# Four graph layers on one core: attention scores from turned gathered rows with 64 target columns, and the edge rows for the scatter assembled in DRAM during the attention

## The reference

```
def _L0_gnn_ref(h, src, dst, Wq, Wk, Wv, Wo, gamma, beta):
    score = jnp.einsum('ehd,ehd->eh', Q[src], K[dst]) / np.sqrt(D)      # H = 4 heads
    attn = jax.nn.softmax(score, axis=1)
    m = V[src] * attn[:, :, None]
    h_new = jax.ops.segment_sum(m, dst, num_segments=n)
    ...
# layer 1: two Chebyshev convolutions, each with two products by the (weighted) adjacency matrix
        return jnp.zeros((n, h.shape[1]), h.dtype).at[row].add(w[:, None] * h[col])
# layer 2: message passing with the 100000 x 64 edge features
    message = jax.nn.relu(node_feats[edge_index[1]] + edge_feats)
    message_reduce = jax.ops.segment_sum(message, edge_index[0], num_segments=num_nodes)
# layer 3: a GAT layer over the same edges
```

## Time and profile before

| | us |
|---|---|
| median of three runs (lowest, highest) | 3534.71 (3491.54, 3550.27) |
| the profiled execution, its span | 3529.8 |
| PE / DVE / ACT / POOL busy in it | 1964.1 / 2235.0 / 1128.3 / 1615.5 |

### The profile page before, as it was taken

The page is one execution under the profiler, slowest core; times in us unless marked ns, Lnnn a source line. Parts: engine busy times, 40 slices in busy tenths (PEclk is TensorE's granted clock), DMA queues, the critical chain, the costliest instruction groups (busy, mean ns, idle before and its releaser), DMA issues. The chain is left out here.

```text
span 3529.8 us, 59565 instructions
## 1 busy us (share of the span) xinstructions
PE 1964.1 (56%) x16222; PEld 1430.6 (41%) x16222; DVE 2235.0 (63%) x4872; ACT 1128.3 (32%) x3658; POOL 1615.5 (46%) x1665
## 2 busy tenths in 40 slices
PE   6844555555555555545766556564545445564487
PEld 5723333333333333334344435453434434554222
DVE  7877777777777777754521112134547557987899
ACT  1144555444444444533210111000001001117544
POOL 1055555555555555553666666645666562000000
PEclk9955555555555555556767677675657657985699
DMA  7912121121212222236222222215544432220000
GB/s 240 364 40 45 42 45 43 43 43 44 45 40 45 42 45 41 45 88 224 65 49 50 50 50 48 60 44 154 147 132 145 127 81 84 85 82 0 0 0 9
DMA packets 399309, 267.13 MB, mean 76 GB/s; under 512 B 321456, under 2 KB 349293, under 8 KB 399073
## 3 DMA queue, kind: packets, MB, share of 16 engines
q1 hardware_dynamic: 306278, 87.81, 11.6%
q10 hardware_dynamic: 41472, 118.96, 9.3%
q0 software_dynamic: 51488, 59.40, 6.7%
HBM read 158.59 MB, written 107.47 MB: 75 GB/s over the span
## 5 line engine op out<-in xcount | busy, mean ns | idle before, releaser
L1254 POOL DMA_INDIRECT sorted_edges<-r_load,r_to x800 | 818.6, 1023 | 544.9 <-SPq L1188 310.2
L807 POOL DMA_INDIRECT hsrc<-h,edges x808 | 775.7, 960 | 593.8 <-PE ps L1004 362.4
L1004 PE MATMUL ps<-AO,hsrc 125*64 125x64 f32 x1616 | 195.9, 316 | 309.9 <-remote 254.3
L1049 PE MATMUL ps<-hot,lo 125*128 125x400 bf16 (+2 forms) x1000 | 272.8, 455 | 100.5 <-DVE hot L866 79.9
L1004 PEld LDWEIGHTS ps<-AO,hsrc 125*64 125x64 f32 x1616 | 180.0, 224 | 345.8 <-issue 345.8
L1031 PE MATMUL ps<-rwin,there 120*125 120x256 bf16 x800 | 183.2, 404 | 235.3 <-DVE there L850 220.0
L875 DVE TENSOR_TENSOR prod<-ps,hsrc 125x1024 f32<-125x1024 f32 x200 | 244.3, 1222 | 105.1 <-issue 101.0
L1572 ACT ACTIVATE w_work<-w_work 128x384 f32<-128x384 f32 (+1 forms) x160 | 85.8, 536 | 701.5 <-DVE w_work L1773 530.4
L866 DVE TENSOR_SCALAR hot<-ramp,small 125x400 bf16<-125x400 int16 x800 | 211.9, 322 | 148.0 <-issue 142.7
L1426 PE MATMUL ps<-R 128*128 128x64 bf16 x3000 | 156.6, 218 | 184.5 <-DVE R L1762 115.9
L1031 PEld LDWEIGHTS ps<-rwin,there 120*125 120x125 bf16 x800 | 145.1, 209 | 274.1 <-issue 274.1
(11 more groups left out here) (412 smaller groups left out, 4187.1 us busy)
## 6 DMA issues: line engine op xcount, KB each, us to landing
w_work<-sorted_edges ACTq DMA_DIRECT2D x42, 1000.0 KB
r_load<-in_edge_attr_dram SPq DMA_DIRECT2D x80, 312.5 KB
dstrow<-dst_rows SPq DMA_DIRECT2D x101, 234.4 KB
sorted_edges<-A ACTq DMA_DIRECT2D x10, 2000.0 KB, 9.7
A<-counts SPq DMA_DIRECT2D x12, 1600.0 KB
counts<-A ACTq DMA_DIRECT2D x4, 4000.0 KB, 29.8
sorted_edges<-A ACTq DMA_DIRECT2D x15, 1000.0 KB, 9.5
hsrc<-h,edges POOLq DMA_INDIRECT x808
```

The lines of the kernel that those rows point to most:

```text
L807: g.indirect_dma_start(out=hsrc[:, s, t, :], out_offset=None, in_=S.h0[:, :], in_offset=bass.IndirectOffsetOnAxis(ap=edges.bitcast(I32)[:, ...
L1004: mm = pe.matmul(sums.rearrange("d (h w) -> d h w", h=H)[:, :, OFF[t]:OFF[t] + SUB], hsrc[0:TP, s, t, :], AO[0:TP, t, :, :], start=(t == 0 ...
L1049: mm = pe.matmul(S.ps[:, at0 + c0:at0 + c1], lo[0:TP, s, t, :], hot[0:TP, t, c0 - k0:c1 - k0], start=(t == FIRST[k]), stop=False, skip_gro ...
L1254: g.indirect_dma_start(out=S.sorted, out_offset=bass.IndirectOffsetOnAxis(ap=to[:, hf, t:t + 1], axis=0), in_=load[:, hf, t, :], in_offset ...
```

## The change

1. **Front.** R is kept transposed (`RT`, f32, 128 partitions x heads x nodes) in place of three bf16 parts. Per block of nodes, two PE products in place of one, one ACT copy in place of two, and no DVE subtractions (`rem`, `low`). The table goes to DRAM as `rt` (6.6 MB in eight DMAs; before 4.8 MB in two). A table `edge_places` of source, target and place per edge (600 KB) replaces two of 800 KB and 400 KB, and `dst_rows` is gone.
2. **Scores.** For each item PE turns the gathered rows (4 transposes), ACT copies them to SBUF (`hT`), and PE multiplies each tile of 125 edges with the 16 x 4 = 64 columns of its 16 nodes (8 f32 products, `rwin` now 128 partitions x 4 x 40 words). DVE picks the edge's own node of 16 with `at` (two products of 125 x 256) and sums over the 16 (one reduction). `there`, `dstrow` and ACT's sums are gone.
3. **Loops.** The attention's loops run over four items (Q = 4), with four slots for `spot`, `edges` and `hsrc`, so POOL may gather up to three items ahead.
4. **Staging.** In the first 20 of its 25 rounds of four items, SP issues `stage_chunk` after each second item: four DMAs from DRAM to DRAM (twice 1250 x 256 B of features and 1250 x 12 B of numbers and places) that assemble one chunk's rows in `staged_edges`.
5. **Scatter.** `bring_half` is one DMA of 128 x 2680 B from `staged_edges`; a row is 67 words, not 80, in the scatter, in the clearing of the table and in the message loop's loads.

```diff
-KW = SP3 * W
+Q = 4
...
-ROW = D + 16
+ROW = D + 3
...
                     c = b - 1
                     act.wait_ge(q["r"], c + 1)
-                    act.copy(R3[:, c, 0, :], S.bank[4 + c % 3][:, 0:H * D]).then_inc(q["hi"], 1)
-                    act.wait_ge(q["rem"], c + 1)
-                    act.copy(R3[:, c, 1, :], rest[:, c % KQ, :]).then_inc(q["mid"], 1)
+                    act.copy(RT[:, :, c * P:(c + 1) * P], S.bank[4 + c % 3][:, 0:2 * P].rearrange("p (k n) -> p k n", k=2)
+                             ).then_inc(q["rt"], 1)
...
+            def kept(b0, b1):
+                act.wait_ge(q["rt"], b1)
+                for half in range(2):
+                    for k in range(2):
+                        act.dma_start(S.rt[half * D:(half + 1) * D, k:H:2, PAD + b0 * P:PAD + b1 * P],
+                                      RT[k * D:(k + 1) * D, :, b0 * P:b1 * P]).then_inc(q["stored"], 16)
...
+                        pe.wait_ge(q["rt"], n - 2)
+                    for k in range(2):
+                        mm = pe.matmul(S.bank[4 + n % 3][:, k * P:(k + 1) * P], Mk[0:D, k * P:(k + 1) * P], HT[0:D, n % KQ, :],
+                                       start=True, stop=True)
+                    mm.then_inc(q["r"], 1)
...
-def bring_half(nc, I, S, sp, c, hf):
-    part = slice(hf * HALF, (hf + 1) * HALF)
-    by_edge = "(p t) f -> p t f"
-    sp.dma_start(S.load[0:TP, hf, :, 0:D], I["edge_attr_64"][bass.ds(c * CE, CE), :].rearrange(by_edge, t=TC)[:, part, :]
-                 ).then_inc(S.landed[hf], 16)
-    with nc.allow_non_contiguous_dma(reason="two node numbers behind each row of features"):
-        sp.dma_start(S.load[0:TP, hf, :, D:D + 2], S.pairs[bass.ds(c * CE, CE), :].rearrange(by_edge, t=TC)[:, part, :]
-                     ).then_inc(S.landed[hf], 16)
-    sp.dma_start(S.to[:, hf, :], S.pos[:, bass.ds(c * TC + hf * HALF, HALF)]).then_inc(S.landed[hf], 16)
+def bring_half(S, sp, c, hf):
+    sp.dma_start(S.load[:, hf, :, :], S.staged[bass.ds(c, 1), hf].rearrange("c p t w -> (c p) t w")).then_inc(S.landed[hf], 16)
+def stage_chunk(nc, I, S, sp, c):
+    by_edge = "(p h t) f -> h p t f"
+    for hf in range(2):
+        rows = S.staged[bass.ds(c, 1), hf, 0:TP].rearrange("c p t w -> (c p) t w")
+        sp.dma_start(rows[:, :, 0:D], I["edge_attr_64"][bass.ds(c * CE, CE), :].rearrange(by_edge, h=2, t=HALF)[hf]).then_inc(S.settled, 16)
+        with nc.allow_non_contiguous_dma(reason="two node numbers and a place behind each row of features"):
+            sp.dma_start(rows[:, :, D:D + 3], S.trip[:, bass.ds((c * 2 + hf) * (HALF * 3), HALF * 3)].rearrange("p (t k) -> p t k", k=3)
+                         ).then_inc(S.settled, 16)
...
-            def line(g, i):
-                sp.wait_ge(q["there"], i + 1)
-                sp.dma_start(dstrow[:, :], S.dst16[bass.ds(g * GE, GE)].unsqueeze(0).to_broadcast([KW, GE])).then_inc(q["dstrow"], 16)
-            with sp.Fori(0, n) as j:
-                for s in range(2):
-                    i = j * 2 + s
-                    g, b = begin(i, s)
-                    sp.wait_ge(q["window_free"], i + 1)
-                    sp.dma_start(rwin[:, s, :], S.r3[bass.ds(b, W)].rearrange("n s c -> (n s) c")).then_inc(q[f"rwin{s}"], 16)
-                    line(g, i)
+            def bring(i, s):
+                b = begin(i, s)
+                sp.wait_ge(q["window_free"], i + 1)
+                sp.sem_inc(q["carrier"], 1)
+                sp.dma_start(rwin[:, s % 2, :, :], S.rt[:, :, bass.ds(b, W)]).then_inc(q[f"rwin{s % 2}"], 16)
+            with sp.Fori(0, C2 // 2) as j:
+                for s in range(Q):
+                    bring(j * Q + s, s)
+                    if s % 2 == 1:
+                        stage_chunk(nc, I, S, sp, j * 2 + s // 2)
+            with sp.Fori(C2 // 2, n) as j:
+                for s in range(Q):
+                    bring(j * Q + s, s)
...
+            sp.wait_ge(S.settled, C2 * 64)
-                bring_half(nc, I, S, sp, 0, hf)
+                bring_half(S, sp, 0, hf)
...
-            with g.Fori(0, n) as j:
-                for s in range(2):
-                    i = j * 2 + s
-                    gather(i + 1, 1 - s, j * 16 + 16 + 16 * s)
+            with g.Fori(0, quads_of(g)) as j:
+                for s in range(Q):
+                    i = j * Q + s
+                    g.wait_ge(landed[s], j * 16 + 16)
+                    g.wait_ge(q["ao_free"], i + 1)
+                    g.sem_inc(q["carrier"], 1)
+                    for t in range(T):
+                        g.indirect_dma_start(out=hsrc[:, s, t, :], out_offset=None, in_=S.h0[:, :],
+                                             in_offset=bass.IndirectOffsetOnAxis(ap=edges.bitcast(I32)[:, s, 4, t:t + 1], axis=0)
+                                             ).then_inc(got[s][t // HT], 16)
...
-                    def products(hf):
-                        v.tensor_tensor(prod[0:TP, :].rearrange("p (t h f) -> p t h f", t=HT, h=H),
-                                        S.ps[0:TP, hf * 1024:(hf + 1) * 1024].rearrange("p (t h f) -> p t h f", t=HT, h=H),
-                                        hsrc[0:TP, s, HT * hf:HT * (hf + 1), :].unsqueeze(2).to_broadcast(four),
-                                        ALU.mult).then_inc(q["scores_free"], 1)
...
-                    keys(0, 4)
-                    products(0)
-                    keys(4, 8)
-                    summed = sums(0)
-                    products(1)
-                    summed = sums(1)
...
+                    v.wait_ge(q["scores"], i + 2)
+                    for r in range(2):
+                        v.tensor_tensor(prod[0:TP, r:T:2, :, :], scores_at(odd, r).rearrange("p (u h w) -> p u h w", u=HT, h=H),
+                                        at[0:TP, r:T:2, :].unsqueeze(2).to_broadcast([TP, HT, H, SUB]), ALU.mult).then_inc(q["scores_free"], 1)
+                    v.wait_ge(q["scores_free"], 2 * i + 6)
+                    own.step(v.tensor_reduce(s4, prod[0:TP, :, :, :], AX.X, ALU.add))
+                    own.step(v.tensor_reduce(top, s4, AX.X, ALU.max))
+                    v.tensor_tensor(s4, s4, over(top, [TP, T, H]), ALU.subtract).then_inc(q["soft"], 1)
...
-            def add(n, hf):
-                act.wait_ge(q["summed"], 2 * n + hf + 1)
-                for c in range(HT * H - BYACT, HT * H):
-                    op = nc.scalar.activation(prod[0:TP, c * D:(c + 1) * D], prod[0:TP, c * D:(c + 1) * D], ACT.Copy,
-                                              accum_out=score[:, hf * HT * H + c:hf * HT * H + c + 1])
-                op.then_inc(q["summed"], 1)
...
-                    add(i, 0)
-                    add(i, 1)
+                for s in range(Q):
+                    act.wait_ge(q["turned"], i + 1)
+                    act.wait_ge(q["scores"], i + 1)
+                    act.copy(hT[:, :, :], S.bank[2 + odd][:, 0:HT * TP].rearrange("p (u e) -> p u e", u=HT)).then_inc(q["moved"], 1)
...
+                    bring_sums(i, j * (Q // 2) + s // 2, odd)
                     act.wait_ge(q["soft"], i + 1)
                     nc.scalar.activation(expo, score, ACT.Exp).then_inc(q["expo"], 1)
-                    rows(i + 1, 1 - s, j * 16 + 16 + 16 * s)
...
-                    pe.wait_ge(q["there"], i + 2)
+                    pe.wait_ge(q["moved"], i + 1)
+                    for u in range(HT):
+                        if u % 2 == 0:
+                            pe.wait_ge(got[s][u // 2], j * (16 * HT) + 16 * HT)
+                        mm = pe.transpose(S.bank[2 + odd][:, u * TP:(u + 1) * TP],
+                                          hsrc[0:TP, s, 2 * u:2 * u + 2, :].rearrange("p t f -> p (t f)"), S.ident[0:TP, 0:TP])
+                    mm.then_inc(q["turned"], 1)
+                    pe.wait_ge(q[f"rwin{odd}"], pair * 16 + 16)
+                    pe.wait_ge(q["scores_free"], 2 * i + 2)
+                    pe.wait_ge(q["moved"], i + 3)
                     for t in range(T):
-                        mm = pe.matmul(S.ps[0:TP, t * 256:(t + 1) * 256], there[:, t * TP:(t + 1) * TP], rwin[:, s, :],
-                                       start=True, stop=True, skip_group_check=True)
-                        if t % HT == HT - 1:
-                            mm.then_inc(q["scores"], 1)
-                    pe.wait_ge(q["scores"], 2 * i + 2)
+                        rows = slice(t % 2 * D, t % 2 * D + D)
+                        mm = pe.matmul(scores_at(odd, t % 2)[:, t // 2 * H * SUB:(t // 2 + 1) * H * SUB], hT[rows, t // 2, :],
+                                       rwin[rows, odd, :, OFF[t]:OFF[t] + SUB], start=True, stop=True, skip_group_check=True)
+                    mm.then_inc(q["scores"], 1)
+                    pe.wait_ge(q["scores"], i + 2)
-                    weigh(i, 1 - s)
+                    weigh(i, (s - 1) % Q)
...
-                    g.wait_ge(S.landed[hf], c * 48 + 48)
+                    g.wait_ge(S.landed[hf], c * 16 + 16)
```

(2 more changed lines are left out.)

317 lines of the change are left out of this document (124 added, 193 removed).

## The result

The change makes the kernel slower where it was measured: 4171.7 us (median of four runs, 4164.4 to 4186.1) against 3539.7 us before (3491.5 to 3550.3), a ratio of 1.187 with an interval of 1.179 to 1.194. The forecast was 3195 us with 2950 to 3440. The forecast was wrong in sign. A chip on which the kernel before takes about 3500 us or more is called stalling from here on, one on which it takes about 3100 us quiet.

What follows compares the result with a forecast made beforehand. No engine was full: the attention was a ring of waits with SP nearly full, and SP's loads stalled scatter and products. Front -5, attention -61, products -171 and the message loop made -340 us: 3195 us, range 2950 to 3440.

Steps and rivals of the forecast that it cites:

- Front: Stage before the attention: fewer DVE subtractions and ACT copies against a larger stored table, -5 us, bounds -21 and +15.
- Attention, engines other than SP: Attention: with four slots POOL no longer waits for `weigh`; POOL and PE bound it at about 10.5 us per item, 1050 us.
- rival C: Attention: engines get no new instructions while SP issues long staging DMAs; 340 to 456 us more, total up to 3712; chance 0.07.
- Attention, SP: Attention: SP's staging DMAs set 13.5 us per item for 80 items, then 10.2 us; 1284 us, 61 less than before.
- the ring: Attention, two slots: gathers wait for the slot's last user, which waits for softmax, which waits for gathered rows; 13.45 us per item.
- Scatter: Scatter: one load replaces three, POOL's 2.6 us stall per half goes; first 46 halves take 634 us in place of 753.9.
- POOL's stall at 2361 is gone: Scatter: its first 46 halves end at 2145 us, after the products (2122), so POOL no longer stalls there.
- Chebyshev products: Products beside the scatter: the stall comes with SP's issuing and falls with one load per half; 398 us, 171 less.
- The stall starts and ends with SP's three loads: Chebyshev products: the argument against rival B, that PE's stall follows SP's loads and not POOL's ten scatters.
- rival B: Products and message loop: stalls come from POOL's scatters or row traffic, not SP's issues; products stay 569 us, total 3423; chance 0.20.
- Message loop: Message loop: starts 237 us earlier, 18.2 us per item beside the scatter, 13.13 behind it; last load at 2820, not 3160.

Runs made afterwards that it cites:

- b5c_no_scatter: The kernel before without POOL's 800 scatters, SP's loads kept, on quiet chip 4: 2768 us beside 3129 us for the kernel before.
- b5d_no_scatter: The kernel before without POOL's 800 scatters, SP's loads kept, on stalling chip 1: 3020 us beside 3517 us for the kernel before.
- e3_q2: The changed kernel with loops over two items and two slots in place of four, on chip 0: 4322 us.
- e6_pause: The changed kernel with POOL clearing a small tile seven times (4.2 us) after every ten scatters, on quiet chip 8: 3406 us.
- e1_ring2: The changed kernel with each gather held back until `weigh` of the item two before is done, four slots kept, on chip 0: 4395 us.
- b7_row67: The kernel before with only its rows cut from 80 to 67 words, on quiet chip 7: 3168 us beside 3099 us for the kernel before.
- after: The changed kernel itself, in its trace on the result's chip: 4171.7 us, ratio 1.187 to the kernel before.
- c3_after: The changed kernel again, on stalling chip 1: 4167 us, ratio 1.186 to the kernel before.

## Why the prediction was wrong, step by step

**The failed step in short.** The sum lets POOL's gathers and scatters run beside the other engines at no price. Measured, an engine that hangs on PE's signals hardly gets on beside them, on the chip of the result. Forecast and measured by part, us: front -5 and +5; attention -61 and +357; transposes and degrees nothing and +282; products -171 and -125; message loop -103 and +124.

**Front, -5 us.** The first AO stands at 232.7 us in place of 227.2: +5, inside its bounds. (`edge_places` is 1.2 MB, 100000 rows of 12 B, and not 600 KB as the list of changes has it.)

**Attention, engines other than SP.** "POOL (10.0 us) and PE (10) could both be the bound, at about 10.5 us" is right on a quiet chip (10.15 to 10.2 in the last 20 items, and in all items without staging) and wrong by half where it was measured: 15.2 us. The failed step is that I let POOL's gathers lie beside the others' work. The row that spoke against it was there: PE's 191 us of unnamed waits, once per round. Before `weigh` PE waits for the signal of its own products of L1031, and that comes about 4 us late; in `b5c_no_scatter`, on a quiet chip, PE has no unnamed wait there. I had the row only in rival C. The work is less, as forecast (DVE 715 us for 1002); where PE's signals come late while POOL gathers, an item costs POOL's 10 us and a part of the others' time one after the other.

**Attention, SP.** I took the issue of a DMA as independent of its pieces, at 2.1 us. It is 0.3 to 0.6 us for small ones and 3.3 to 4.3 us for 1250 pieces. The forecast pace of 13.5 us under staging came out at 13.9 and 14.4 us on the quiet chips and 13.9 without gathers, since the two errors (small ones too dear, large ones too cheap) cancel. On the stalling chip it was 17.6. I also overlooked that `rwin`, still with two slots, stands ahead of the next `edges` on SP, which keeps the ring in another place.

**Scatter.** "The 2.6 us stall per half goes": it did, to one of 4.4 to 5.1 us in three halves; the first 46 halves took 674 us (634 forecast), and a later chunk 28.5 (28.3 forecast). "POOL's stall at 2361 is gone": it grew from 30 us to 270, since the scatter came to its wait for the products when 10 of their 100 blocks were done. That the short stalls were of use on such a chip I did not see: PE ran in them and behind them.

**Transposes and degrees.** They have no term in my sum, and grew by 282 us. I had looked at the stages in which SP's loads could be seen, and not asked what POOL's unbroken scatter does to the first stage beside it. In the kernel before POOL stood still there for 41 us at a stretch (until 1637). That this pause is what kept them short is argued, from the stage's late signals.

**Chebyshev products.** -171 forecast, -125 measured, and that is luck. The whole gain is in the 90 blocks that ran while POOL stood (3.0 us each); the 10 beside a scatter with one load per half took 16.6 us each, not 6.2. "The stall starts and ends with SP's three loads" was a true reading of the earlier trace rows and no cause: `b5d_no_scatter` keeps the loads and loses the stall. The end of SP's loads and POOL's pause fall together, because the loads are what made POOL pause. That was rival B's mechanism, to which I gave 0.20 and only as a lost gain. Its sum was wrong as well: if the scatters are the cause, a scatter without pauses makes the stages beside it dearer.

**Message loop.** 18.2 us per item beside the scatter forecast; measured are 68 us (the loads from 2959.7 to 3367.2 us, six intervals), and 13.15 us per item behind it, as forecast. This is the same error.

**Rival C**, the slower one, had the right direction and size (8.2 us more per pair of items, where it counted 8.5 to 11.4) and the wrong culprit: SP's staging, and instructions that don't come. The bodies' 218 and 217 instructions are also fewer than the two blocks of 256 that it counts, so by its own rule they stay loaded, and no code is fetched in 1300 us of this attention. The staging lost 159 us of the 344 lost in the attention on chip 1, `e3_q2` shows that the length of the bodies is no large part, and 0.07 was far too little for a stall that two rows of the trace showed.

**What stays open.** Why chips 0 and 1 (and the one of the result) stall and chips 4, 7 and 8 do not; whether pauses put into POOL's scatter would help on a stalling chip (`e6_pause` came on a quiet one); what delays PE's signals there (late code is excluded for the attention); and whether the stall is there in an execution of which nothing is recorded. `e3_q2` against `e1_ring2` excludes most of the body's length.

## What to carry to other kernels

Where an engine trickles in step with something, there are often two things in that step: take each away by itself before one is called the cause. Where the profile can't name who ended a wait, look up in the code which signal it was and whose: here it was PE's own. And treat a wait that is about to be removed as possibly useful to others. Count a DMA's pieces when it is priced on its queue, and prefer to put small fields into place on chip (POOL's 0.2 us copy) over 1250 pieces of 8 or 12 B. A change of this kind is to be timed on several chips: its sign differed here.

## What the runs showed of the hardware

- The same program took 3491 to 3632 us on some chips and 3099 to 3130 us on others. The stages that differ are those beside POOL's indirect DMAs: 13.5 against 11.0 us per item beside gathers, 561 against 289 us (`b7_row67`) for the products beside scatters; the message items behind the scatter have 13.1 us on both.
- On the slower chips signals of PE come up to 42 us behind its instructions beside POOL's indirect DMAs, and never over 1.9 us behind where these are left out; on the others they come within 0.15 us. Signals of DVE and ACT are in time in both (the changed kernel).
- In 1300 us of the changed kernel's attention loop there is no packet of code on the DMA queues (`after`, `c3_after`).
- A DMA of 1250 pieces holds the next one on SP's queue for 2.2 to 4.5 us (2.2 and 2.9 in `b5d_no_scatter`, 3.2 to 4.5 in the staging), with pieces of 8, 12 and 256 B; one of 128 pieces for less than 0.6 us.
- Rows of 268 B in place of 320 B made the old kernel slower (3168 against 3099 us, one run of each), though they are fewer bytes.
